# Six shared-expert groups between the two routings of the top-4 layers, and other conditions for GpSimd's waits

## The reference, cut to what matters

```
scores = softmax(flat @ router_w.T + router_bias)             # 32 experts
topk_scores, topk_idx = top_k(scores, 4)                      # normalised to sum 1
h = silu(flat @ gate_w[e].T) * (flat @ up_w[e].T)             # expert e, hidden 128
out = sum over the 4 chosen e of topk_score * (h @ down_w[e].T)
out = out + silu(flat @ sgate_w.T) * (flat @ sup_w.T) @ sdown_w.T   # shared expert, hidden 512
x = x + 0.5 * out
```

## Time and profile before

| | us |
|---|---|
| median of 3 runs | 1732.25 (1725.69 to 1733.0) |
| the profiled execution's own time | 1729.27 |
| its span in the profile | 1727.4 |
| busy: PE, DVE, POOL, ACT | 1176.4, 1020.9, 790.3, 672.2 |
| mean granted clock of PE | 0.845 of full speed |

### The profile page before, as it was taken

One profiled execution on the slowest core, in us unless ns is written; L12 is line 12 of the kernel. 1 busy time (PEld: TensorE's weight loads), 2 busy tenths in 40 slices (PEclk: granted clock), 3 DMA queues, 4 the chain that ended last, 5 costly groups with the idle time before them and its releaser, 6 DMA issues.

```text
span 1727.4 us, 31813 instructions
## 1 busy us (share of the span) xinstructions
PE 1176.4 (68%) x10584; PEld 857.3 (50%) x10585; DVE 1020.9 (59%) x2671; ACT 672.2 (39%) x1035; POOL 790.3 (46%) x989
## 2 busy tenths in 40 slices
PE   2198578885298108698966458888884095989762
PEld 2098456664298103597952123444443034979620
DVE  6546667777446893233565757888867931335533
ACT  2054256773054002254532136767761022545310
POOL 0523435562524257666667532222200476666676
PEclk9999699996599559799987658999995597999986
DMA  9233134430132001465631100000000014646422
GB/s 366 67 94 108 45 102 162 159 106 1 60 94 75 18 33 50 144 196 160 195 113 49 37 14 2 2 0 0 0 1 1 29 50 132 200 159 198 135 61 62
DMA packets 100090, 150.12 MB, mean 87 GB/s; under 512 B 21520, under 2 KB 54928, under 8 KB 99216
## 3 DMA queue, kind: packets, MB, share of 16 engines
q1 hardware_dynamic: 58768, 75.30, 13.5%
q0 software_dynamic: 20480, 41.98, 8.4%
q10 hardware_dynamic: 20736, 31.47, 5.4%
HBM read 74.16 MB, written 74.45 MB: 86 GB/s over the span
## 4 chain that ended last, share of the span: by engine, by line
PE 36%; POOL 19%; DVE 17%; issue 13%; DMA 8%; ACT 3%; SPq 2%; DVEq 0%; ACTq 0%; POOLq 0%
POOL AREA L1098 10%; POOL slots_top L624 9%; PE PS L908 5%; PE PS L845 5%; DMA AREA<-results_top,ROW 4%; PE PS L930 3%; PE PS L298 3%; PE PS L300 2%; PE PS L299 2%; DVE AREA L1961 2%; PE PS L1789 2%; DVE XN L407 2%; PE PS L1776 2%; PE PS L1764 2%; SPq L1346 2%
## 5 line engine op out<-in xcount | busy, mean ns | idle before, releaser
L624 POOL DMA_INDIRECT slots_top<-XN,ROW x320 | 317.3, 992 | 362.5 <-DVE ROW L578 221.1
L1098 POOL DMA_INDIRECT AREA<-results_top,ROW x320 | 304.7, 952 | 243.3 <-DMA results_top<-AREA 89.4
L1009 DVE SCALAR_TENSOR_TENSOR AREA<-PS,AREA 128x512 f32<-128x512 f32 x96 | 66.4, 692 | 233.2 <-ACT AREA L983 232.9
L908 PE MATMUL PS<-WGU,AREA 128*128 x768 | 188.3, 389 | 0.0
L1961 DVE TENSOR_REDUCE AREA<-PS 128x4 f32<-128x1024 f32 x128 | 156.8, 1225 | 38.0 <-PE PS L1764 35.2
L1881 ACT ACTIVATE AREA<-PS,AREA 128x1024 f32<-128x1024 f32 x128 | 142.8, 1116 | 83.8 <-PE PS L1776 81.8
L908 PEld LDWEIGHTS PS<-WGU,AREA 128*128 128x128 f32 x768 | 142.7, 196 | 17.1 <-ACT AREA L972 0.7
L417 PE MATMUL PS<-IDF,XN 128*128 128x128 f32 x192 | 49.0, 414 | 129.0 <-DVE XN L407 129.0
L1379 POOL TENSOR_TENSOR AREA<-AREA 128x1536 f16<-128x1536 f32 x32 | 92.9, 2903 | 85.9 <-ACT AREA L1594 85.9
L930 PEld LDWEIGHTS PS<-WD,AREA 128*128 128x128 f32 x768 | 100.2, 191 | 12.7 <-DVE AREA L1004 8.2
L930 PE MATMUL PS<-WD,AREA 128*128 x768 | 102.0, 276 | 6.3 <-DVE AREA L1004 6.3
(11 more groups left out here) (257 smaller groups left out, 3114.8 us busy)
## 6 DMA issues: line engine op xcount, KB each, us to landing
AREA<-slots_top SPq DMA_DIRECT2D x96, 256.0 KB, 3.1
results_top<-AREA ACTq DMA_DIRECT2D x96, 256.0 KB, 2.3
slots_top<-ZERO SPq DMA_DIRECT2D x24, 512.0 KB, 3.4
AREA<-slots_top SPq DMA_DIRECT2D x48, 128.0 KB, 2.3
results_top<-AREA ACTq DMA_DIRECT2D x48, 128.0 KB, 2.4
AREA<-query_rows SPq DMA_DIRECT2D x48, 128.0 KB, 2.8
slots_top<-XN,ROW POOLq DMA_INDIRECT x320, 2.2
AREA<-results_top,ROW POOLq DMA_INDIRECT x320, 2.6
```

The costliest lines, as they stand in the source:

```text
L624: nc.gpsimd.indirect_dma_start(out=L.xs[q], out_offset=bass.IndirectOffsetOnAxis(ap=ROW[:, n:n + 1], axis=0), in_=XN[:, t * D:(t + 1) * D] ...
L908: ins = nc.tensor.matmul(o, XTF[:, v, j * P:(j + 1) * P], w, start=True, stop=True)
L1009: nc.vector.scalar_tensor_tensor(out=HF[:, v, :4 * P].rearrange("p (j h) -> p j h", h=P), in0=got, scalar=1.0 / SX, in1=HA[:, :4 * P].rear ...
L1098: nc.gpsimd.indirect_dma_start(out=slots[L.tag][u][:, c * D:(c + 1) * D], out_offset=None, in_=L.ys[g * GT // L.tiles], in_offset=bass.Ind ...
```

## The change

The first six shared groups, not four, are worked on early, and they stand between the routing of part 0 and the routing of part 1 in the programs of PE, ACT and DVE. They use other scratch (`YG`, `YS`) and PSUM bank 6 in place of 3, so that what the routing of part 1 needs stays. Only shared groups 6 and 7 are left for the tail. SP's and PE's conditions for the first expert step (all of both routings) stay as they are.

POOL no longer waits for its own transfers to land. In the dispatch it waits, before every 8 transfers, for shared groups (part 0) or expert steps (part 1); in the gathers of groups 0 to 3 for expert steps of part 1, and before group 7 for shared group 6.

```diff
+EARLY = 6
@@ route_vector
                 route_part(dve, L, q, link)
+                if L is L1 and q == 0:
+                    shared_vector(dve)
@@ dispatch_pool
+        def keep_step(pool, q, chunk):
+            if q == 0 and chunk > 1:
+                pool.wait_ge(*sh_h.at(SC * min(chunk - 1, EARLY)))
+            if q == 1 and chunk > 2:
+                pool.wait_ge(*bl_h.at(3 * (chunk - 2)))
...
+                if L is L1 and n % 8 == 0:
+                    keep_step(pool, q, n // 8 % 8)
                 nc.gpsimd.indirect_dma_start(
...
-                every = (16, 8)[q] if L is L1 else (0, 4)[q]
-                if every and n % every == every - 1:
+                if L is L0 and q == 1 and n % 4 == 3:
                     pool.wait_ge(*dp_sent[q].at(16 * (n % (L.tiles * L.K) + 1)))
@@ shared groups
-            for g in range(half * NG // 2, (half + 1) * NG // 2):
+        def shared_early(group):
+            for g in range(EARLY):
                 group(g)
+        def hidden_gate(g):
+            return YG[:, 0:1024] if g < EARLY else HA
+        def down_rows(g):
+            return YS[:, 0, :] if g < EARLY else XTF[:, 0, :]
+        def up_bank(g, j):
+            return (2, 6 if g < EARLY else 3)[j % 2]
@@ shared_tensor
-            pe.wait_ge(*rt_tab.at(L1.parts))
+            pe.wait_ge(*rt_tab.at(1))
...
-                group(NG // 2 + i)
+                if NG // 2 + i >= EARLY:
+                    group(NG // 2 + i)
@@ combine_pool
+                    if L is L1 and g < NG // 2 and c % 8 == 0 and 2 * g + c // 8 > 1:
+                        pool.wait_ge(*bl_h.at(L.part_steps + 3 * (2 * g + c // 8 - 1)))
+                    if L is L1 and g > max(EARLY, NG // 2) and c == 0:
+                        pool.wait_ge(*sh_h.at(SC * g))
                     got = cb_tile[c // L.K] if L is L1 and g == NG - 1 else cb_got[u]
                     nc.gpsimd.indirect_dma_start(
...
-                    if L is L1 and c % 8 == 7 and (g < NG // 2 or c < GK - 1):
-                        landed = L.turn[g] * GK + c + 1 if got is cb_got[u] else c % L.K + 1
-                        pool.wait_ge(*got.at(16 * landed))
@@ scalar program
-                    route_scalar(act, L)
+                    route_scalar(act, L, [0])
+                    if L is L1:
+                        shared_scalar(act, 0)
+                    route_scalar(act, L, range(1, L.parts))
...
-                        act.wait_ge(*rt_row.at(L.parts))
-                        shared_scalar(act, 0)
@@ vector program
-                    if L is L1:
-                        shared_vector(dve)
@@ tensor program
-                    route_tensor(pe, L)
+                    route_tensor(pe, L, [0])
                     if L is L1:
                         shared_tensor(pe, 0)
+                    route_tensor(pe, L, range(1, L.parts))
```

More of the change, by code:

```diff
@@ L471, in build, with route_tensor @@
         LN_COUNTS = {ln_stat: NT, ln_norm: NG, ln_hi: NG, ln_tr: NG, ln_xt: NG}
-        def route_tensor(pe, L):
-            for q in range(L.parts):
+        def route_tensor(pe, L, parts):
+            for q in parts:
                 pe.wait_ge(*rt_choice.at(q + 1))
@@ L600, in route_steps, with route_scalar @@
             return L.parts * (5 + (0 if L.K == 1 else 2) + 3 + 5 + 2 + 2 + 2 + 2 * L.K + 5 + (7 if L is L1 else 0))
-        def route_scalar(act, L):
+        def route_scalar(act, L, parts):
             if L is L1:
                 ex = EX[:, :L.ET]
-                for q in range(L.parts):
+                for q in parts:
                     for n, v in enumerate((ex, W4[:, q * L.tiles:(q + 1) * L.tiles, :])):
@@ L644, in shared_tensor @@
             pe.wait_ge(*w_down.at(80))
[L645 removed]
+            pe.wait_ge(*rt_tab.at(1))
             def up(g, j):
                 wait(pe, sh_h, g * SC + j - 1)
[L649 removed]
+                for b, w in ((j % 2, SG), (up_bank(g, j), SU)):
                     ins = product3(banks(b), [w[h][:, j * P:(j + 1) * P] for h in range(2)],
@@ L670, in group @@
             def group(g):
-                later = g % (NG // 2) != 0
+                later = g not in (0, EARLY)
                 for j in range(SC):
@@ L678, in shared_tensor @@
             if half == 0:
-                shared_groups(0, group)
-                down(NG // 2 - 1)
-                turned(NG // 2 - 1)
+                shared_early(group)
+                down(EARLY - 1)
+                turned(EARLY - 1)
                 return
@@ L700, in columns @@
                 wait(act, sh_y, g)
-                nc.scalar.activation(turned_rows, banks(4), ACT.Copy).then_inc(sh_tc.sem, 1)
+                nc.scalar.activation(down_rows(g), banks(4), ACT.Copy).then_inc(sh_tc.sem, 1)
             def group(g):
@@ L705, in group @@
                     n = g * SC + j
-                    if j == 3 and g % (NG // 2) != 0:
+                    if j == 3 and g not in (0, EARLY):
                         columns(g - 1)
@@ L709, in group @@
                     wait(act, sh_h, n - 1)
-                    nc.scalar.activation(HA[:, (j % 2) * GC:(j % 2 + 1) * GC], banks(j % 2), ACT.Silu,
+                    nc.scalar.activation(hidden_gate(g)[:, (j % 2) * GC:(j % 2 + 1) * GC], banks(j % 2), ACT.Silu,
                                          scale=1.0 / (SX * SW)).then_inc(sh_silu.sem, 1)
             if half == 0:
-                shared_groups(0, group)
-                columns(NG // 2 - 1)
+                shared_early(group)
+                columns(EARLY - 1)
                 return
@@ L739, in shared_group_vector @@
                 wait(dve, sh_t, g - 1)
-                nc.vector.scalar_tensor_tensor(out=HS[:, g % 2, j * GC:(j + 1) * GC], in0=banks(2 + j % 2),
-                                               scalar=1.0 / (SX * SW), in1=HA[:, (j % 2) * GC:(j % 2 + 1) * GC],
+                nc.vector.scalar_tensor_tensor(out=HS[:, g % 2, j * GC:(j + 1) * GC], in0=banks(up_bank(g, j)),
+                                               scalar=1.0 / (SX * SW), in1=hidden_gate(g)[:, (j % 2) * GC:(j % 2 + 1) * GC],
                                                op0=ALU.mult, op1=ALU.mult).then_inc(sh_h.sem, 1)
-            if g % (NG // 2) != 0:
+            if g not in (0, EARLY):
                 shared_add(dve, g - 1)
         def shared_vector(dve):
-            shared_groups(0, lambda g: shared_group_vector(dve, g))
-            shared_add(dve, NG // 2 - 1)
+            shared_early(lambda g: shared_group_vector(dve, g))
+            shared_add(dve, EARLY - 1)
         def blocks_sync(sp, L):
```

8 lines of the change are left out of this document (3 added, 5 removed).

## The result

The changed kernel takes 1704.5 us, the median of four runs (1699.67 to 1709.0), against 1732.2 for the kernel before on the same chip; the ratio is 0.9835, 95% interval 0.9806 to 0.9864. The forecast was 1702. The profiled execution is one of the longer ones, 1707.96 us with a span of 1706.2 (before: 1729.27 and 1727.4), so the traces show 21.2 us of the 27.7.

The account below looks back on a forecast made before the run. PE held 36% of the chain, but POOL's gathers (10%) and dispatch (9%) in the top-4 layers were the target. Layer gains −13.2 and −15.1 sum to −28.3 from 1729.27, 1701.0, stated as 1702; range 1693 to 1715.

Parts of the forecast that it names:

- First load, +2.2: SP's first load, behind six early groups and then the routing of part 1, goes out 2.2 us later, at 706.2.
- ACT's table, +0.5: Two further ACT table loads per layer; the one before the first expert silu costs 0.5 us (0 to 1.3).
- Boundary, −6.1: On PE between parts 0 and 1: load wait gone (−4.4), with the clock kept up −6.5; taken as −6.1 us.
- End of the steps, −3.4: End of part 1's expert steps: first load, table and boundary together give −3.4 us (−0.9 to −4.3).
- Gathers: POOL's part 0 gathers take 80 us without landing waits; part 1's stores release group 4 at 889.4 and 1626.7.
- Tails: Ends of the top-4 layers: first −13.2 us, nearest to the DVE bound; second −15.1 us, through POOL's gathers.
- marks for the second layer: Signs in the second layer: group 4's first gather released near 1627, last gather landed near 1708.
- the boundary's gap: Rival: loads for part 1 still come late and PE waits between parts; sum −16, 1713 us; chance 0.14 with binding waits.
- the slow early groups: Rival: early shared groups run on a slow PE clock, over 9.15 us each; 1738 to 1811 us; chance 0.05.
- The landing waits were paid for something: Rival: POOL's queue can't take 64 transfers in a row, so waits return as longer issues; −3, 1726 us; chance 0.09.

Follow-up runs that it names:

- the last run: Changed kernel with four early groups and, in part 0's dispatch, one POOL wait after 8 transfers until all four end: 1750.3 us, ratio 1.012 to the kernel before.
- the version without waits: Changed kernel without its new POOL waits for groups and steps, landing waits also out: 2233.7 us, ratio 1.076 to the kernel before on a slow chip.

## Why the prediction was right

It was right in time, sign and mechanism on the chip it was made for. That the single stages moved as forecast is read from the two traces. By its own steps:

- **First load, +2.2:** +1.45. Routing of part 1 ends at 705.09 + 0.22, the sum said 706.2. The early groups had the forecast pace, 9.15 us.
- **ACT's table, +0.5:** nothing. ACT loads the Silu table while PE still works on the first products, and the silu waits 1.7 us more for these after the load. ACT's groups by line, 705 to 715:

```profile
L1007 ACT ACT_TABLE_LOAD x1 | 1.3, 1283 | 0.0
L1007 ACT ACTIVATE AREA<-PS 128x512 f32<-128x512 f32 x1 | 0.6, 598 | 1.7 <-PE PS L932 1.7
```

The time that the Trainium skill gives for a switch ("ScalarE: Activation LUTs", "What ACT_TABLE_LOAD costs"), 2.66 us, isn't seen: the load is 1.28 us and hidden here, and where nothing hides it (a load at 1009.10, in attention) the next activation starts 0.01 us after it, 1.31 us after the end of the one before.

- **Boundary, −6.1:** the transposes follow at once and the clock stays up, as said: transposes 1.04 for 1.98, products 1.99 for 3.40. The first DVE product behind it comes at 802.02 for 806.59 (−4.6); with +1.45 ahead of it that is a step of −6.0. By the rule of the Trainium skill ("TensorE: Matmul & The Clock Gate", "Part 1: The HAM clock gate") −6.5 was due; the rows lie nearer to −6.1. The idle gap and the low clock are both gone; what is left is 0.88 us in which PE waits for ACT's copy of the transposed slots (L996).
- **End of the steps, −3.4:** last store at 885.36 for 889.9, **−4.5**, because the table load cost nothing and the first load was earlier.
- **Gathers:** group 4 at 888.13, forecast 889.4; in the second layer it is 15.2 earlier (1620.15 for 1635.38), 5.9 of them from the earlier start (1347.53 for 1353.45) and 9.3 of its own (8.7). The prediction's marks for the second layer, 1627 and 1708, leave out that the first layer's gain moves everything behind it; its sum adds the two gains and is not touched by this. No landing wait came back as a longer issue: 64 take 79.9 us, forecast 80.
- **Tails:** group 4 combined at 909.63 (910.7); first layer −16.0 (−13.2), second −15.3 (−15.1). The 2.8 us more in the first are 1.1 of earlier steps and 1.7 of a shorter DVE tail (71.2 us from the combining of group 4 to the load, before 74.4; forecast 1.5 less, it was 3.2).
- **What the sum lacked:** attention. It took for granted that untouched code keeps its time; 10.1 us came back there in the profiled execution; the two shorter runs, at a higher clock, have no trace. Between the profiled executions the layers gave 31.3 us where 28.3 were forecast, and 21.2 were left. Between the medians it is −27.7. That this lies within 1 us of the forecast is partly luck: the layers' surplus and attention's loss have opposite signs.
- **The starting point:** the 28.3 were taken from the profiled 1729.27, not from the median; from the median 1732.2 the same sum gives 1703.9, nearer to the measured 1704.5 than the stated 1702.

Of the rivals, the boundary's gap and the slow early groups didn't show. "The landing waits were paid for something" is false on the chip of the result, and true on the slow ones, but by another mechanism than the one priced: issues don't get longer (the gaps in long runs stay at 0.30 us), signals of PE to ACT and DVE come late. On one of the slow chips the waits taken out alone cost 5.4%. On the chip of the result no single part of the change was run alone, so the split between order and waits rests on the trace, and no run there shows that the new waits are needed.

## What to carry to other kernels

Before pauses are taken out of a long run of indirect transfers, see whether other engines lag beside it: where PE's signals came late, taking the pauses out cost 5 to 8% against the kernel before, while a version with waits for the lagging work, in the same set, was level with it (0.9995). Pauses of both kinds together did no worse on another such chip. Read the stage that a transfer feeds, as here, to see whether its landing is what ends last; then 27 us are a sum of two boundaries and two tails. And measure on more than one chip: on a slow chip four early groups beat the change's six by 1.8%, which no run has tried as such on a chip like that of the result (the last run has a pause besides).

## What the runs showed that was not expected

- The same kernel before takes 1732 and 1733 us on two chips and 2074 to 2118 on three others. On the one of these three with a profile of it, most of the difference is in the top-4 layers (2 × 140 us of some 400).
- On the slow chips signals from PE reach ACT up to 23 us late in the rows above, and DVE too, while POOL issues indirect transfers, and promptly from some 10 us after it stops: the silus' late waits add to 222 us in the version without waits, and "another core or an unknown queue" holds 23% of its chain, 0% on the chip of the result. Signals from ACT to DVE stay prompt (0.03 us above), and so do the transfers' own landings (POOL waits 1.54 us for one at 687.91 in the kernel before, as in the earlier trace rows). That the transfers cause it is argued from when it begins and ends; the run that was to stop them beside the groups fell on a chip without the effect, so it isn't shown, nor is by what path it happens.
- Attention's 2820 matmuls took 265, 268 and 276 us of PE in three profiles of equal code (the kernel before, the last run, the changed kernel), at granted clocks of 0.83, 0.81 and 0.79.
